# Keys and values of a head convolved in one pass on half the array's rows

## The reference

```
gx    = x.reshape(8, 64, 64, 64)            # 8 heads of 64 channels
query = gconv3x3(gx, qw)                    # 3x3, 4 groups of 16 channels, SAME
key   = gconv3x3(gx, kw)
value = gconv3x3(gx, vw)
h, w  = mean of query over rows, over columns; cat(h, w) through a 1x1 convolution
gated = gx * sigmoid(g_h) * sigmoid(g_w)
qn    = (gated - mean) * rsqrt(var + eps) * gnw + gnb     # per channel
out   = softmax(qn.T key / 16) value        # 4096 x 4096 scores per head
```

## Time and profile before

| | us |
|---|---|
| median of 3 runs | 8617.35 (8609.17 to 8619.54) |
| profiled execution, its own time | 8605.12 |
| its span | 8603.4 |
| mean granted TensorE clock | 0.948 |
| PE busy over the span | 7662.7 (89%) |
| first convolution matmul starts | 38.38 |
| attention phase issues its first load | 591.55 |

### The profile page before, as it was taken

One profiled execution on the slowest core, in us unless ns is written; L12 is line 12 of the kernel. 1 busy time (PEld: TensorE's weight loads), 2 busy tenths in 40 slices (PEclk: granted clock), 3 DMA queues, 4 the chain that ended last, 5 costly groups with the idle time before them and its releaser, 6 DMA issues. The chain is left out here.

```text
span 8603.4 us, 139512 instructions
## 1 busy us (share of the span) xinstructions
PE 7662.7 (89%) x42791; PEld 4610.2 (54%) x42948; DVE 6045.4 (70%) x8270; ACT 4604.1 (54%) x7731; POOL 5937.8 (69%) x4067
## 2 busy tenths in 40 slices
PE   8979999999999997699999999999999997775993
PEld 3437777777777775244344444344444433554882
DVE  2227777777777776499999999898999997560116
ACT  1126767766676774456566665566666654221223
POOL 0007777777777773499999999999999997322005
PEclk9989999999999997799999999999999999887996
DMA  1120000101101004211112111112211111333213
GB/s 60 49 88 0 25 0 25 25 0 25 25 0 25 5 0 141 89 60 60 63 67 69 65 66 52 64 66 68 69 62 58 62 64 46 133 112 131 66 54 123
DMA packets 174420, 487.18 MB, mean 57 GB/s; under 512 B 31766, under 2 KB 70324, under 8 KB 151984
## 3 DMA queue, kind: packets, MB, share of 16 engines
q1 hardware_dynamic: 159024, 442.56, 15.5%
q10 hardware_dynamic: 8960, 25.17, 0.7%
q0 software_dynamic: 6144, 16.33, 0.6%
HBM read 360.72 MB, written 123.73 MB: 56 GB/s over the span
## 5 line engine op out<-in xcount | busy, mean ns | idle before, releaser
L1454 DVE TENSOR_TENSOR_SCAN hh<-mb_ps_da,state,hh 128x512 f32<-128x512 f32 x2048 | 2489.5, 1264 | 126.8 <-POOL hh L1367 74.3
L1367 POOL TENSOR_TENSOR hh<-dtx,bb 128x1024 f32<-128x1024 f32 x1024 | 2401.5, 2373 | 224.8 <-PE mb_ps_y L1116 220.5
L620 POOL TENSOR_TENSOR p_lo<-p_turned 128x512 bf16<-128x512 f32 x2048 | 2065.7, 1041 | 588.7 <-ACT p_turned L584 572.6
L1257 ACT ACTIVATE mb_ps_da<-dt,amat 128x512 f32<-128x512 f32 x2048 | 1392.1, 686 | 1342.8 <-DVE hh L1454 1335.9
L1116 PE MATMUL mb_ps_y<-hh,ident 128*128 128x512 f32 x4096 | 1980.6, 611 | 19.1 <-POOL hh L1373 12.1
L638 DVE TENSOR_SCALAR_CACHE_REDUCE prob<-ps_s 128x1024 f32<-128x1024 f32 x1024 | 1213.3, 1222 | 388.0 <-PE ps_s L519 387.8
L527 PE MATMUL ps_t<-ident,prob 128*128 128x128 f32 x8192 | 1309.7, 282 | 3.4 <-issue 2.7
L1116 PEld LDWEIGHTS mb_ps_y<-hh,ident 128*128 128x128 f32 x4096 | 792.3, 195 | 966.3 <-issue 859.3
L584 ACT ACTIVATE p_turned<-ps_t 128x512 f32<-128x512 f32 x1280 | 763.3, 596 | 809.4 <-PE ps_t L527 809.4
L578 ACT ACTIVATE prob<-prob,nmx 128x1024 f32<-128x1024 f32 x1024 | 1165.8, 1141 | 29.5 <-DVE nmx L643 28.4
L1461 DVE TENSOR_TENSOR hh<-hh,mb_ps_c 128x1024 f32<-128x1024 f32 x768 | 922.0, 1200 | 260.0 <-PE mb_ps_c L1105 193.8
(11 more groups left out here) (224 smaller groups left out, 7863.1 us busy)
## 6 DMA issues: line engine op xcount, KB each, us to landing
bb<-mb_bc SPq DMA_DIRECT2D x128, 1024.0 KB, 4.7
cc<-mb_bc SPq DMA_DIRECT2D x256, 256.0 KB, 3.1
q_head<-q_full SPq DMA_DIRECT2D x16, 1024.0 KB, 16.8
mb_u<-u SPq DMA_DIRECT2D x32, 512.0 KB, 3.3
m_dirs<-mo SPq DMA_DIRECT2D x32, 512.0 KB, 8.4
ex_w<-in_L_ffn_w SPq DMA_DIRECT2D x16, 1024.0 KB, 7.7
xbuf<-ml_zero SPq DMA_DIRECT2D x16, 640.0 KB, 5.5
ex_xr<-xbuf SPq DMA_DIRECT2D x40, 256.0 KB, 2.7
```

The costliest lines, as they stand in the source:

```text
L620: pool.tensor_tensor(lo[:, k % RING, :], pt[:, k % RING, :], hi_view[:, k % RING, 1::2], ALU.subtract).then_inc(lo_ready, 1)
L1257: act.activation(ps_da[:, exp_bank(e), :], dt[:, j, blk, :], ACT.Exp, scale=amat[:, j, blk, r % S:r % S + 1]).then_inc(da_ready, 1)
L1367: pool.tensor_tensor(hh[:, r % RING], dtx[:, j, half(r // S)], bb[:, r % S, :].unsqueeze(1).broadcast_to([P, HK, CH]), ALU.mult).then_inc( ...
L1454: dve.tensor_tensor_scan(h, a, h, state[:, s.j, q % S, blk:blk + 1], ALU.mult, ALU.add).then_inc(scanned, 1)
```

## The change

Keys and values of one head are computed in one pass: the stationary operand is now 64 rows (the head's channels) by 128 columns (64 key channels, then 64 value channels), and the two heads of a pair use the upper and the lower half of the array's rows, in alternating matmuls into different PSUM banks. ACT copies both results to `kvimg[pair % 2][head]`, where keys lie on partitions 0 to 63 and values on 64 to 127. The values are turned from there with transposes of 64 rows, two for each 128 pixels. There are no separate value chunks: 32 chunks in all, each with keys and values, and the transposes of a chunk follow the convolution of the next. The queries come after the second chunk of a pair, the 1x1 convolution and the next pair's group means after the fourth. The other work of ACT and DVE is spread over the chunks anew.

POOL clears the weights first and of the padded images only the rims, and DVE begins once `group8` is made. SP issues only the 16 DMAs of the key and value weights; ACT issues the other 16. The keys are stored in two DMAs of 64 partitions each, the values in two halves, and the second half of the values goes out behind the keys.

```diff
-    wq, wk, wv = sb("wq", [P, 9, P]), sb("wk", [P, 9, P]), sb("wv", [P, 9, P])
+    wkv, wq = sb("wkv", [P, 9, P]), sb("wq", [P, 9, P])
-    kimg = sb("kimg", [P, L])
+    kvimg = [[sb(f"kvimg{j}{h}", [P, L]) for h in range(2)] for j in range(2)]
+    ps_kv = ctx.enter_context(nc.psum_tensor("ps_kv", [P, 2, 2, CH], F32))
@@ pool
-            for t in (wq[:, :, :], wk[:, :, :], wv[:, :, :], wc1[:, :], xpads[0][:, :, :], xpads[1][:, :, :], colsum[:, :, :], rowsum[:, :, :]):
-                pool.memset(t, 0.0).then_inc(zeroed, 1)
+            for t in (wkv, wq):
+                pool.memset(t[:, :, :], 0.0).then_inc(w_zeroed, 1)
+            pool.memset(wc1[:, :], 0.0).then_inc(w_zeroed, 1)
...
+            for t in xpads:
+                for edge in (0, PAD - 1):
+                    pool.memset(t[:, edge, :], 0.0).then_inc(strips, 1)
+                    pool.memset(t[:, 1:PAD - 1, edge:edge + 1], 0.0).then_inc(strips, 1)
@@ sync
+            for i in range(PAIRS):
+                if i + 1 < PAIRS:
                     sp.wait_ge(xn_ready, ONE + i + 1)
                     load(i + 1)
+                for half in range(2):
+                    if half:
+                        sp.wait_ge(kv_ready, ONE + 2 * NCH * (i + 1) + 2)
+                        for h in range(2):
+                            sp.dma_start(k_full[i * P + DH * h:i * P + DH * h + DH, :], kvimg[i % 2][h][0:DH, :]).then_inc(k_stored[i % 2], 16)
+                    sp.wait_ge(v2_ready, ONE + i * NCH + (half + 1) * HALF + 2)
+                    ts = slice(half * QT // 2, (half + 1) * QT // 2)
+                    sp.dma_start(v_split[2 * i:2 * i + 2, :, half * QT // 2 * P:(half + 1) * QT // 2 * P].rearrange("h p n -> p h n"),
+                                 vparts[:, :, ts, :].rearrange("p h t c -> p h (t c)")).then_inc(v_stored[half], 16)
                 sp.wait_ge(q_ready, ONE + i + 1)
+                sp.dma_start(q_full[i * P:(i + 1) * P, :], gated[:, :]).then_inc(q_stored, 16)
@@ tensor
+            def keys_and_values(n):
+                i, c = divmod(n, NCH)
+                if c == 0:
+                    pe.wait_ge(xn_ready, ONE + i + 1)
+                pe.wait_ge(kv_ready, ONE + 2 * n)
+                for t in range(9):
+                    dy, dx = divmod(t, 3)
+                    for h in range(2):
+                        mm = pe.matmul(ps_kv[:, c % 2, h, :], wkv[rows[h], t, :],
+                                       xpads[i % 2][rows[h], 8 * c + dy:8 * c + dy + 8, dx:dx + IMG],
+                                       start=(t == 0), stop=(t == 8))
+                        if t == 8:
+                            mm.then_inc(kv_summed, 1)
+            def turn_values(n):
+                i, c = divmod(n, NCH)
+                pe.wait_ge(kv_ready, ONE + 2 * n + 4)
+                pe.wait_ge(v2_ready, ONE + n + 1)
+                for t in range(4):
+                    px = slice(c * CH + t * P, c * CH + (t + 1) * P)
+                    for h in range(2):
+                        last = pe.transpose(ps_v[:, n % 2, t * P + h * DH:t * P + h * DH + DH],
+                                            kvimg[i % 2][h][rows[1], px], ident[rows[1], rows[1]])
+                last.then_inc(v_turned, 1)
+            for n in range(CHUNKS):
+                i, c = divmod(n, NCH)
+                keys_and_values(n)
+                if n == 1:
+                    pe.wait_ge(w_ready, ONE + 16 * N_CONV_W)
+                if c == 1:
+                    queries(i)
+                if c == 3:
+                    pe.wait_ge(cat_ready, ONE + i + 1)
+                    pe.matmul(mixed, wc1[:, :], cat[:, :], start=True, stop=True).then_inc(c1_done, 1)
+                if c == 3 and i + 1 < PAIRS:
+                    group_means(i + 1)
+                if n:
+                    turn_values(n - 1)
+            turn_values(CHUNKS - 1)
@@ scalar
+            for n in range(CHUNKS):
+                evacuate(n)                    # two copies ps_kv -> kvimg, 128x512 each
+                if n:
+                    high_parts(n - 1)          # ps_v -> vparts, 128x512, one copy
+                if c == 1:
...
+                if c == 3:
...
+                if c == 4 and i + 1 < PAIRS:
+                    normalize(i + 1)
+                if c == 6:
...
@@ vector
+                if g == 1 and i + 1 < PAIRS:
+                    channel_moments(i + 1)
+                if g == 2:                     # first multiplication by the gates
...
+                if g == 3:                     # group_affine(i + 1), second multiplication
...
+                if g == 4:                     # statistics of the gated image
...
+                if g == 6 and i + 1 < PAIRS:
+                    column_sums(i + 1)
+                if g == 5:                     # final scale, then row_sums(i + 1)
...
```

More of the change, by code:

```diff
@@ L118, in conv_phase @@
     var2_ready, std2_ready, qaff_ready = sem("var2_ready"), sem("std2_ready"), sem("qaff_ready")
[L119 to L122, removed]
+    kv_summed, kv_ready, v_turned = sem("kv_summed"), sem("kv_ready"), sem("v_turned")
+    v1_ready, v2_ready, q_ready = sem("v1_ready"), sem("v2_ready"), sem("q_ready")
+    rows = [slice(DH * h, DH * h + DH) for h in range(2)]
     inner = [t[:, 1:IMG + 1, 1:IMG + 1] for t in xpads]
     image = lambda t: t[:, :].rearrange("p (h w) -> p h w", w=IMG)
[L126 to L135, removed]
+    CHUNKS = PAIRS * NCH
+    HALF = NCH // 2
+    STRIPS = 11
     start_semaphores()
@@ L166, in _ @@
                     n += 1
[L167 to L176, removed]
+            assert n == N_CONV_KV_W
+            for i in range(PAIRS):
+                if i + 1 < PAIRS:
@@ L202, in group_means, with queries @@
                 pe.matmul(ps_g[:, :], group8[:, :], chan[:, :], start=True, stop=True).then_inc(grp_summed, 1)
[L204 to L217, removed]
+            def keys_and_values(n):
[11 more added lines that the diff above has]
+                            mm.then_inc(kv_summed, 1)
+            def queries(i):
                 pe.wait_ge(sums_ready, ONE + 2 * (i + 1))
+                if i:
+                    pe.wait_ge(gates_ready, ONE + i)
                 for t in range(9):
@@ L226, in step @@
                 last.then_inc(q_summed, 1)
[L227 to L250, removed]
@@ L300, in _, with evacuate @@
-            normalize(0, 0, True)
-            act.wait_ge(w_ready, ONE + 16 * N_CONV_W)
-            pairs(act, step)
+                act.activation(inner[i % 2], image(ximg), ACT.Identity, scale=col[:, 1:2], bias=col[:, 2:3]).then_inc(xn_ready, 1)
+            def evacuate(n):
+                i, c = divmod(n, NCH)
+                if c == 0 and i >= 2:
+                    act.wait_ge(k_stored[i % 2], ONE + 32 * (i // 2))
+                for h in range(2):
+                    act.wait_ge(kv_summed, ONE + 2 * n + h + 1)
+                    act.activation(kvimg[i % 2][h][:, c * CH:(c + 1) * CH], ps_kv[:, c % 2, h, :], ACT.Copy).then_inc(kv_ready, 1)
@@ new lines, in high_parts @@
+            def high_parts(n):
+                i, g = divmod(n, NCH)
+                if g % HALF == 0 and i:
+                    act.wait_ge(v_stored[g // HALF], ONE + 16 * i)
+                act.wait_ge(v_turned, ONE + n + 1)
+                act.activation(vparts[:, :, 4 * g:4 * g + 4, 0:DH],
+                               ps_v[:, n % 2, :].rearrange("p (t h c) -> p h t c", t=4, h=2),
+                               ACT.Copy).then_inc(v1_ready, 1)
+            n = 0
+            act.wait_ge(w_zeroed, ONE + 3)
@@ new lines, in _ @@
+            for j in range(8):
+                act.dma_start(wq[16 * j:16 * j + 16, :, 16 * j:16 * j + 16], qw[j % 4]).then_inc(w_ready, 16)
+                n += 1
+            for h in range(2):
+                act.dma_start(wc1[rows[h], rows[h]], c1w).then_inc(w_ready, 16)
+                for j, v in enumerate((c1b, gnw, gnb)):
+                    act.dma_start(vecs[rows[h], j:j + 1], v.unsqueeze(1)).then_inc(w_ready, 16)
+                n += 4
+            assert n == N_CONV_W
+            act.wait_ge(strips, ONE + STRIPS)
```

214 lines of the change are left out of this document (90 added, 124 removed).

## The result

The changed kernel's median is 8352.16 us (8346.19 to 8358.0, 4 runs), that of the kernel before 8614.99 us (4 runs). The ratio is 0.9695, with a 95% interval of 0.9678 to 0.9712: 262.8 us faster. The profiled execution has a span of 8344.4 us (forecast 8359.8).

What follows compares the result with a forecast made beforehand. PE was taken to bound the convolution phase, whose end moves the time one for one: -247.1 - 12.7 + 13.1 + 1.6 + 1.5 = -243.6 from 8617.35 gave 8373.7 us, 8 in 10 within 8350 to 8406.

Steps and rivals of the forecast that it cites:

- Row halves side by side: Convolutions: two row halves run at once, 576 pairs of records at 0.429 us each, saving 247.1 us.
- Transposes: Value turning: eight half-row transposes per chunk, not side by side, taken at 0.11 us each, +13.1 us.
- my other bound: Value transposes: if half the columns cost half, eight cost what the four did, adding 0.
- rows 8: Profile rows of narrow query matmuls, 64 moving columns: 36 records in 3.96 us, 0.11 each, used to price transposes.
- Start: Phase head: PE's first convolution at 25.7 us instead of 38.4, -12.7 us.
- Order of ACT and DVE: Beside PE's chunks: group means, normalizing, query sums and next image load all fit in time, none ends last.
- rival 1: Convolution phase: a moved step stops PE, late images and scalings cost 27 us, giving 8401; chance 0.11.
- Tail: Last chunk's end to attention's first load: 25.6 us against 24.1, +1.5, with keys stored at half rate.
- the loads' rows: Profile rows pricing key stores: loads into 64 partitions move 205 GB/s, a store of all 444.
- rival 4: Convolution phase: half rows keep PE at 1.2 GHz, +294 us on -243.6, giving 8668; chance 0.04.
- Visits of full-row matmuls: Query, 1x1 and group matmuls interrupt half-row ones: 0.1 us into and out of each of eight visits, +1.6 us.
- The rest: Attention and everything later: as long as before, 8011.9 us.

Runs made afterwards that it cites:

- Experiment 1: Changed kernel with nine taps of head 0, then nine of head 1, instead of heads alternating at every tap: 8548.37 us.
- Experiment 3: Changed kernel with values turned by plain f32 matmuls with the identity instead of transposes, on the same half rows: 8397.58 us.
- experiment 4: Changed kernel with start undone in three runs: images cleared whole, 8363.19 us; all small DMAs on SP, 8342.03; whole old start, 8364.19.
- experiment 2: Changed kernel with heads alternating every three taps instead of every tap: 8375.4 us, one run.
- experiment 6: Changed kernel plus keys stored in halves, queries ahead of the last halves, and head 1's keys and values swapped between partition halves: 8335.0 us, again 8342.72.
- experiment 7: Kernel of experiment 6 plus first image loaded in two halves and head 1's keys stored from ACT's queue: 8345.78 us, again 8343.52.

## Why the prediction was right

- **Row halves side by side**: right, and the gain's cause. Forecast -247.1; 18 pairs of a chunk take 7.72 us. Experiment 1 takes 194.6 of it away by order alone. The rest stays because PE reaches four records ahead, which I had not considered: 4 x 0.429 us in each of 31 chunks are 53.
- **Transposes**: one behind the other on one half, as said, but of the wrong size; the largest error. I took 0.11 us each, by the query matmuls, and they take 0.063; a chunk cost 8.28 and not 8.6, 30 x 0.32 = 9.6 us. The eight take 0.50, close to the 0.44 that my other bound gave (half the columns, half the time). Experiment 3 shows that the kind matters: rows 8 are plain f32 matmuls, with a weight load of 0.19 us, and the trace before already had 0.14 for a transpose's, which I passed over. The row that was nearest in shape was not nearest in kind.
- **Start**: forecast 25.7, measured 26.20. The two causes were named right, and the second queue rightly given no share of its own (experiment 4).
- **Order of ACT and DVE**: rival 1 did not come. DVE's statistics ended at 64.2 for group means that PE took at 65.46, and no later image was waited for. Behind the first convolution PE waited 0.5 us, in the tail.
- **Tail**: forecast 25.6, measured 337.32 - 312.28 = 25.0. Keys went at 210 GB/s against 438, as the loads' rows had it.
- **Clock** (rival 4): it did not come. In the changed kernel the granted clock is 1.00 from 31 us to beyond the last convolution (first line below), so half rows kept the higher level. In experiment 3 it fell once (second line), for 3.4 us and with PE busy all the time, behind 6 us of queries and turnings by matmul; in the other pairs the same work passed at 1.00, and the cause is open. It cost 1.7 us of that run's first load.

```profile
30.00:320.00 290.00, 283.64 (x1558) 229.84 (x1556) 145.74 (x164) 92.14 (x126) 0.00 (x0) 1.00 0.29 92
...
293.50:296.80 3.30, 3.30 (x12) 2.02 (x11) 0.69 (x1) 0.77 (x2) 0.00 (x0) 0.50 0.00 0
```

- **Visits of full-row matmuls**: 1.6 forecast. A chunk with queries took 12.59 - 8.28 = 4.31 more than one without, of which the queries are 3.96; one with the 1x1 and group matmuls 0.68 more, of which they are about 0.4. That is 0.3 a visit, 2.4 in all.
- **A term at nothing**: the ends of the pairs. In the kernel before, two groups of transposes stood there one behind the other, with a wait for ACT's copy and for the next keys:

```profile
171.89 0.60 PE L248 MATMUL ps_v<-ident,v_chunk 128*128 128x128 f32 x4
172.74 0.66 PE L248 MATMUL ps_v<-ident,v_chunk 128*128 128x128 f32 x4 [0.25 <-ACT v_chunk L283]
173.23 9.18 PE L214 MATMUL ps_k<-xpad,wk 128*128 128x512 f32 x21
```

  From 171.89 to 173.23 are 1.34 us, of which the eight transposes are 0.88. The other 0.46, three times, had no place in the sum and are gone: a pair's last chunk and the next one's first now lie 8.28 us apart like any others. That is 1.4 us.
- **The rest** (behind the attention's first load) took 8007.1 us in the profiled execution against 8011.9, and the median lay 6 us over it and not 12. Both are chance and not forecast: 11.0 of the 21.5 us by which the median beat the forecast.

Together: the start +0.5; from the first to the last convolution -10.6 (312.28 - 26.20 = 286.1 against 296.65), which are -9.6 for the transposes, +0.8 for the visits, -1.4 for the ends of the pairs and -0.3 for the half clock at the start, which lasted 4.9 us behind the first convolution and 5.5 before; the tail -0.6; the rest -4.8. That is -15.5, and 8359.8 - 15.5 = 8344.3, the measured span. The new kernel also writes out the loop over the pairs, which the old one ran as a loop; no run tries that alone, and the sum closes without it.

## What to carry to other kernels

When a contraction uses half the array's rows, give the other half an independent matmul into another PSUM bank and alternate at every instruction. Here the number of records stayed as it was, and their time halved. Price a small operation by rows of its own kind (transposes by transposes), not by rows of its shape. Of the DMAs at a start, wait only for those the next step reads; and count a store from 64 partitions at half rate (here 210 GB/s against 438) where it ends a phase.

## What the runs showed of the hardware

- Matmuls of one row half start ahead of earlier ones of the other half, about four f32 records ahead (experiments 1 and 2). The convolution record inside the transposes, at 74.25, is the same.
- Eight f32 transposes of 64 rows on one half took 0.50 us, on alternating halves 0.25 (experiment 6). As plain matmuls with the identity they took 1.23 us a chunk more (experiment 3).
- Two key stores at once, from different halves of the partitions on two queues, moved 357 GB/s, one alone 210.
- Mamba, which no version touches, took 3817.2 to 3833.3 us from first to last matmul. In the execution with 3817.2 (the changed kernel) PE stood at 1.2 GHz for 291 us, in the one with 3833.3 (experiment 7) for 321, in that of experiment 4 with the old start (3832.3) for 330, in that of the one queue (3817.3) for 287. Over the fourteen kept traces length and low clock go together (correlation 0.91), though not tightly: experiment 7's second trace had 3832.0 with 312. Which causes which was not tried.
- Two traces of the same version agree better in what follows the first load than traces of different versions do: 8007.1 and 8007.9 for the changed kernel, 8011.7 and 8008.8 for experiment 6, 8023.5 and 8022.0 for experiment 7. So the earlier start of experiment 7 may itself lengthen what follows, by more than it wins. Two traces each don't show it, and it stays open beside plain scatter.
